# Rotation tables gathered once per cosine and sine, and spread over the partitions by ScalarE

## The reference

```python
inv_freq = 1.0 / theta ** (jnp.arange(0, dim, 2) / dim)      # 64 frequencies
freqs = jnp.einsum('i,j->ij', t, inv_freq)                   # 512 positions
emb = jnp.concatenate([freqs, freqs], axis=-1)               # each one twice
cos, sin = jnp.cos(emb)[position_ids], jnp.sin(emb)[position_ids]
q = q * cos + _rotate_half(q) * sin      # rotate_half: [-x2, x1]
k = k * cos + _rotate_half(k) * sin
scores = q @ k.T / sqrt(128)             # masked, softmax, @ v, @ Wo
x = x + tanh(g_xattn) * attention(layernorm(x), ctx)
x = x + tanh(g_ffn) * ffn(layernorm(x))
```

## Time and profile before

| | |
|---|---|
| median of 3 runs | 682.74 us (681.73 to 683.15) |
| the profiled execution | 682.45 us |
| its span, first to last instruction | 680.6 us |
| TensorE busy in the span | 663.5 us |
| TensorE's granted clock | 0.997 of full speed |
| first stage, up to the first scores | 0 to about 121.5 us |

### The profile page before, as it was taken

The page is one execution under the profiler, slowest core; times in us unless marked ns, Lnnn a source line. Parts: engine busy times, 40 slices in busy tenths (PEclk is TensorE's granted clock), DMA queues, the critical chain, the costliest instruction groups (busy, mean ns, idle before and its releaser), DMA issues.

```text
span 680.6 us, 11325 instructions
## 1 busy us (share of the span) xinstructions
PE 663.5 (97%) x3352; PEld 555.4 (82%) x3352; DVE 485.0 (71%) x1223; ACT 321.9 (47%) x903; POOL 385.3 (57%) x323
## 2 busy tenths in 40 slices
PE   7999999999999999999999999999999998999998
PEld 6777888778888888888888888888888886778886
DVE  2788575887777777777777777777777776774433
ACT  4343722554544545445445454454454536766210
POOL 5546766886556666665566666655666655531000
PEclk8999999999999999999999999999999999999999
DMA  9977894232122131213212121221210042000002
GB/s 304 311 242 232 272 309 155 90 97 93 58 83 93 35 105 33 92 31 108 91 32 94 47 92 31 93 70 69 77 33 31 32 155 79 0 1 1 1 31 93
DMA packets 62157, 66.34 MB, mean 97 GB/s; under 512 B 5920, under 2 KB 43808, under 8 KB 62112
## 3 DMA queue, kind: packets, MB, share of 16 engines
q1 hardware_dynamic: 60688, 64.77, 29.4%
q0 software_dynamic: 384, 1.05, 0.5%
q10 hardware_dynamic: 1040, 0.00, 0.1%
HBM read 46.93 MB, written 18.87 MB: 97 GB/s over the span
## 4 chain that ended last, share of the span: by engine, by line
PE 86%; DVE 5%; POOL 3%; ACT 2%; issue 2%; DMA 1%; SPq 0%; DVEq 0%; POOLq 0%; ACTq 0%
PE f_bank L459 10%; PE f_bank L461 10%; PE f_bank L460 10%; PE o_bank L459 9%; PE o_bank L461 9%; PE o_bank L460 9%; PE s_banks L583 6%; PE t_bank L465 4%; PE pv_bank L459 3%; PE pv_bank L461 3%; PE pv_bank L460 3%; PE s_banks L584 2%; PE t_bank L459 1%; PE s_banks L459 1%; PE t_bank L460 1%
## 5 line engine op out<-in xcount | busy, mean ns | idle before, releaser
L1104 POOL TENSOR_TENSOR prob<-prob,small 128x512 f32<-128x512 f32 x64 | 66.7, 1042 | 139.5 <-DVE small L1345 139.5
L864 ACT ACTIVATE prob<-prob,small 128x128 f32<-128x128 f32 x256 | 99.8, 391 | 81.4 <-DVE small L1335 75.9
L795 ACT ACTIVATE o_hi<-pv_bank 128x512 fp32r<-128x512 f32 x64 | 38.5, 601 | 145.7 <-PE pv_bank L461 145.4
L459 PE MATMUL o_bank<-wo_hi,o_hi 128*128 128x512 f32 x256 | 105.7, 413 | 0.0
L459 PE MATMUL f_bank<-xT_hi,wq_hi 128*128 128x512 f32 x256 | 101.5, 396 | 0.0
L461 PE MATMUL o_bank<-wo_hi,o_lo 128*128 128x512 f32 x256 | 100.5, 393 | 0.0
L1060 POOL TENSOR_TENSOR q_lo<-q,q_hi 128x512 fp32r<-128x512 f32 x64 | 82.8, 1293 | 30.6 <-ACT q_hi L795 30.6
L460 PE MATMUL o_bank<-wo_lo,o_hi 128*128 128x512 f32 x256 | 100.0, 391 | 0.0
L461 PE MATMUL f_bank<-xT_hi,wq_lo 128*128 128x512 f32 x256 | 99.8, 390 | 0.0
L460 PE MATMUL f_bank<-xT_lo,wq_hi 128*128 128x512 f32 x256 | 99.8, 390 | 0.0
L1247 DVE TENSOR_TENSOR t_sin<-f_bank,rope 64x512 f32<-64x512 f32 x128 | 88.2, 689 | 2.8
(11 more groups left out here) (180 smaller groups left out, 1468.7 us busy)
## 6 DMA issues: line engine op xcount, KB each, us to landing
k_scratch<-ks_parts SPq DMA_DIRECT2D x16, 512.0 KB, 3.1
raw<-in_L_xattn_Wq_dram SPq DMA_DIRECT2D x32, 256.0 KB, 2.8
raw<-in_L_xattn_Wo_dram SPq DMA_DIRECT2D x32, 256.0 KB, 2.6
k_parts<-k_scratch SPq DMA_DIRECT2D x16, 512.0 KB, 3.6
v_scratch<-vs_hi SPq DMA_DIRECT2D x16, 256.0 KB, 3.7
v_scratch<-vs_lo SPq DMA_DIRECT2D x16, 256.0 KB, 4.0
v_hi<-v_scratch SPq DMA_DIRECT2D x16, 256.0 KB, 3.9
v_lo<-v_scratch SPq DMA_DIRECT2D x16, 256.0 KB, 4.2
```

Source lines behind the costliest of these rows:

```text
L459: nc.tensor.matmul(dst, st[0], mv_[0], start=start, stop=False)
L864: e = nc.scalar.activation(prob[:, k, h, :], prob[:, k, h, :], ACT.Exp, bias=nmin[k][:, h:h + 1], scale=-1.0, accum_out=psum_row[k][:, h:h ...
L1104: nc.gpsimd.tensor_tensor(prob[:, k], prob[:, k], rrow[k].unsqueeze(2).to_broadcast([128, GH, S]), ALU.mult).then_inc(pool_norm, 1)
```

## The change

The gathered row becomes 128 numbers (64 cosines, 64 sines), 512 bytes in place of 1024. One tile of four transposes then holds four batches: cosines on partitions 0 to 63 of the bank and sines on 64 to 127. There are two such tiles in place of four, after blocks 1 and 5, and each is spread into rope by four ScalarE copies of 64 partitions by 512 columns in place of two copies of 128 by 512. The minus sign of the second sine half comes from the copy's scale.

```diff
-TILES_AT = {-1: [("ctx", 0), ("ctx", 1), ("ctx", 2), ("ctx", 3)], 1: [("rope", 0), ("rope", 1)],
-            2: [("ctx", 4), ("ctx", 5), ("ctx", 6), ("ctx", 7)], 5: [("rope", 2), ("rope", 3)],
+TILES_AT = {-1: [("ctx", 0), ("ctx", 1), ("ctx", 2), ("ctx", 3)], 1: [("rope", 0)],
+            2: [("ctx", 4), ("ctx", 5), ("ctx", 6), ("ctx", 7)], 5: [("rope", 1)],
...
-    return np.ascontiguousarray(np.concatenate([c, c, s, -s], axis=1).astype(np.float32))
+    return np.ascontiguousarray(np.concatenate([c, s], axis=1).astype(np.float32))
...
-        rope_tok = place("rope_tok", [128, B, 256], F32, at["pT_hi"])
+        rope_tok = place("rope_tok", [128, B, 128], F32, at["pT_hi"])
...
-                    pe.wait_ge(rope_loaded[2 * b], 16)
-                    pe.wait_ge(rope_loaded[2 * b + 1], 16)
-                    mm = transpose4(tile_bank(t), lambda k: rope_tok[:, 2 * b + k % 2, (k // 2) * 128:(k // 2 + 1) * 128])
+                    for k in range(4):
+                        pe.wait_ge(rope_loaded[4 * b + k], 16)
+                    mm = transpose4(tile_bank(t), lambda k: rope_tok[:, 4 * b + k, :])
...
-                    hi(rope[:, :, b * 256:(b + 1) * 256], tile_bank(t).rearrange("p (two s) -> p two s", two=2), act_tile)
+                    tk = slice(b * HT, (b + 1) * HT)
+                    nc.scalar.activation(rope[0:64, 0, tk], tile_bank(t)[0:64, :], ACT.Copy)
+                    nc.scalar.activation(rope[64:128, 0, tk], tile_bank(t)[0:64, :], ACT.Copy)
+                    nc.scalar.activation(rope[0:64, 1, tk], tile_bank(t)[64:128, :], ACT.Copy)
+                    nc.scalar.activation(rope[64:128, 1, tk], tile_bank(t)[64:128, :], ACT.Copy, scale=-1.0).then_inc(act_tile, 1)
...
                 if fixed and r < 2:
-                    dve.wait_ge(act_tile, tile_of("rope", 1) + 1)
-                elif fixed and r == 2:
-                    dve.wait_ge(act_tile, tile_of("rope", 3) + 1)
+                    dve.wait_ge(act_tile, tile_of("rope", 0) + 1)
+                elif fixed and r == 2:
+                    dve.wait_ge(act_tile, tile_of("rope", 1) + 1)
```

## The result

| | before | changed |
|---|---|---|
| median of 7 runs each | 682.53 us (681.73 to 683.15) | 684.77 us (683.9 to 685.03) |
| ratio to before, 95% interval | | 1.003 (1.0018 to 1.0042) |
| profiled execution, its span | 682.45, 680.6 us | 684.83, 682.9 us |

The changed kernel is 2.24 us slower. That is inside the range of 682.0 to 684.9, but the forecast was 683.6, so the loss is more than twice the 0.9 us that the sum gave. It is also more than the 0.2% that a measurement can tell from no change.

A forecast was written before the change was run, and what follows sets the result against it. TensorE, busy 663.5 of 680.6 us, was taken to bound the kernel, with xnorm's chain deciding the x tile's start. Only the second spread counted, +0.9 us: span 681.5, profiled 683.35, median forecast 683.6 us, range 682.0 to 684.9.

The forecast's parts named there:

- the sum: Transposes 0, gathers 0, first spread 0, second spread +0.9 us: span 680.6 to 681.5, median 683.6 us.
- Transposes, worth 0: TensorE before V2 and V4: eight fewer transposes save 0.88 us of work, but only lengthen waits that something else ends.
- Gathers, worth 0: GpSimd still issues eight gathers of 128 rows at 0.95 us each; fewer bytes gain 0, at most 1.5 us.
- First spread, worth 0: ScalarE's two added copies from about 17 us delay VectorE's K(0,0) products by 0.98 us, which costs nothing.
- The cover: GpSimd's first key sum, held by the gathers until 21.73, leaves 0.46 us after VectorE's delayed products end at 21.27.
- Second spread, +0.95: ScalarE's four copies behind vs_hi of V3 delay VectorE's K(0,1) product from 38.10 to 39.05, with nothing covering it.
- a copy begins about 0.49 us after the one before: Spacing of ScalarE copies, read from 128 partitions and taken for 64: two added copies cost 2 x 0.49 = 0.98 us.
- The other end that it named: Upper bound for the two added ScalarE copies of a spread: 2 x 0.60 = 1.2 us if they didn't overlap.
- The collisions: VectorE and GpSimd block each other around chunks 6 and 7 and the variance's tiny operations, which end 0.9 us later.
- the rival with one collision more: One more variance operation or a pushed-back GpSimd sum makes the chain 1.4 to 1.9 us late: 684.5 us, chance 0.20.
- TensorE itself comes to the x tile at 68.4 ... the wait shrinks to 0.9: TensorE arrives before xnorm's release at 69.2, so the 1.36 us wait shrinks and the x tile begins 0.9 us later.
- A delay or a gain made before that goes to the end unchanged: From 80 us on TensorE is fully busy at full clock, so earlier shifts reach the end in full.

The follow-up runs named there:

- first_two: The changed kernel, but the first tile of the tables is copied by two copies of 128 partitions, without the spread: 684.33 us, ratio 1.0035.
- shared_early: The changed kernel with the second spread ahead of vs_hi of V2, all eight gathers before the weight splits, and VectorE making the first spread's sine copies: 682.13 us.
- norms_early: shared_early with the first four xnorm operations moved on ScalarE to right behind vs_hi of V7: 680.98 us, ratio 0.9971.
- warm_gap: The changed kernel with 18 idle transposes of the identity on TensorE in the pause before K(2,0): 684.03 us, ratio 1.0016.
- early_spread: The changed kernel with the four copies of the second tile moved in ScalarE's list ahead of vs_hi of V2: 682.68 us, ratio 0.9998.
- before_norms: The kernel before the change, with only the first four xnorm operations moved to right behind vs_hi of V7: 681.36 us, ratio 0.9981.

## Why the prediction was right or wrong

**Transposes, worth 0: right, as far as can be measured.** Both waits grew (forecast 0.78 and 1.16, measured 0.89 and 1.01), and doing the transposes twice doesn't change the median (684.83).

**Gathers, worth 0: right.** A gather of 512-byte rows took 0.95 us like one of 1024, and the wide rows cost nothing (684.26). The GpSimd row at 21.36 is the same as in the earlier trace rows apart from the start.

**First spread, worth 0: right, by a hair.** VectorE's products ended at 22.22 (20.83 + 1.39) and GpSimd's sum began at 22.33. The cover was put at 0.46 us with 0.98 for the copies. As these don't overlap, 0.11 us is left between the two. first_two shows the same time as the changed kernel.

**Second spread, +0.95: the right place and the wrong size.** This is the term that was mis-sized. The step was "a copy begins about 0.49 us after the one before", taken over from 128 partitions. The other end that it named, 2 x 0.60 us without overlap, was the true one, and it applies to three of the four copies and to vs_hi behind them. VectorE's product of K(0,1) began at 39.99 in place of 38.10; less the 0.58 us by which the store ahead came later (vs_hi of V3 at 36.97 for 36.39) that is 1.31 us in place of 0.95, so 0.36 more. That is 0.1 above even that other end, since the two copies that were there before are no longer 0.49 us apart either. Why neighbouring copies of this kind don't overlap is open, as said above. Everything downstream is late by about this 0.36 and else as forecast, if V4's 0.41 us is added to the forecast starts: K(2,0) 46.4 + 0.41 = 46.81, measured 47.24; the last tiny operation's end 51.7 + 0.41 = 52.11, measured 52.50; the x tile 69.2 + 0.41 = 69.61, measured 69.96.

By the Trainium skill (ScalarE: Activation LUTs, What ACT_TABLE_LOAD costs) neighbouring ACTIVATEs overlap by 93 ns. The copies of 128 partitions agree (0.60 long, 0.49 apart); those of 64, with starts that change between neighbours, don't (0.59 long, 0.60 apart), and the measurement decides.

**The collisions: right.** VectorE's chunk 7 came in at the boundary between two operations of GpSimd (0.82 us in place of 1.81) and GpSimd's chunk 6 was stretched from 1.28 to 1.71, where 1.76 had been taken. Four of the 12 tiny operations met GpSimd's work, two early and two late, as the forecast had it. So the rival with one collision more names nearly the measured time (684.5) by a mechanism that didn't happen, and that the measured time lies in the range at all, near its upper end, is partly luck: that end was made for collisions, and the loss beyond the chain has another source.

**"TensorE itself comes to the x tile at 68.4 ... the wait shrinks to 0.9": wrong in most profiles.** The step counted the later K(2,0) as 1.4 us that the wait of 1.36 before xnorm takes up. In time it does: with full clock 0.68 us of the wait are left. But the standstill before K(2,0) itself grew from 0.81 to 2.74 us, and in six profiles of seven the clock is halved behind it. Then TensorE, not the chain, arrives last at the x tile, 2.0 us late and not 1.2, of which 0.3 are won back in the transposes. In the kernel before the standstill at this place had full clock behind it, but its profile has the half clock at 8 to 12 us (0.56 and 0.59 in the two stretches), so the prediction could have named it as a rival: a longer pause of TensorE isn't always free, even when a later wait takes it up.

**"A delay or a gain made before that goes to the end unchanged": nearly right.** It rested on one stretch, 80 to 100 us. From the first scores to the end of the span the kernel before needs 559.1 us, and eleven of the other profiles are 0.1 us below that to 0.6 above. The two that aren't, shared_early and norms_early, need 1.7 and 2.3 us more, 1.6 of it behind the standstill at 561 to 563 us.

**The sum, put right**: +1.25 us of the chain with full clock (forecast 0.9 and 0.36 for the copies), which stands on the rows. warm_gap, whose 12 executions have a mean clock of 0.999 or 1.000, loses 1.2 us in the median, just that. The changed kernel loses 2.2 to 2.4, so about 1.0 us are left that warm_gap doesn't have. The half clock behind K(2,0) is 0.4 of it in the profiles at the first scores. The other 0.6 I can't assign: the part behind the first scores differs by as much from profile to profile (the changed kernel's first profile is +1.25 there, +0.41 from its start, and +0.57 behind them). That the half clock is the rest of the loss is thus supported by the count of executions and by warm_gap, and shown by the profiles for less than half.

## What to carry to other kernels

Count the copies of an engine before the bytes or the partitions: four of 64 partitions cost more than twice as much as two of 128 (2.4 us against 1.08), and what the change saved in DMA bytes and in TensorE work ahead of waits was worth nothing that could be measured. Such copies belong in a place where their engine is idle; in early_spread they were free without one instruction less. And where a chain gets later, look at the pause that it tears into TensorE as well as at the wait at its end: the pause can have a price of its own. Where an early gain doesn't reach the end, look at the later standstills and at the clock behind them.

## What the runs showed of the hardware

ScalarE's copies of 128 x 512 out of PSUM are 0.60 us long and 0.48 to 0.49 us apart. Those of 64 x 512 are as long, but whatever follows one starts 0.59 to 0.62 us after its start where nothing else holds it, in each of the forms tried. So half the partitions cost 0.1 us more here, not less. In all these forms the start of what is read or written changed between neighbours, so the partitions alone may not be the reason.

The granted clock of TensorE fell to half behind a standstill of 2.6 to 3.1 us in six profiles of seven, at the same place of the same program once with and once without it (0.50 and 1.00 from 46 to 48 us). Behind standstills up to 1.6 us at that place it stayed full in all seven. But at 561 to 563 us it fell to half behind a standstill of 1.61 us in two profiles (shared_early and norms_early; 0.65 and 0.50 in the stretches from 564 to 568 us of the first), and stayed full behind one of 1.52 us in the other twelve. So the length of one standstill doesn't decide it alone: behind 1.63 us before K(2,0) the clock was full (before_norms). The execution was 1.6 us longer behind that fall, and on average 0.4 us longer at the first scores behind the one at K(2,0).
